# GpSimd normalises the fourth and fifth block's x and makes four low parts of the first two blocks; the engines' programs in a new order

## What is computed

```
x = x + layernorm(attention(layernorm(x)))       # one head: q, k, v from W_qkv, softmax(q k' / sqrt(128)) v
x = x + layernorm(ffn(layernorm(x)))
ffn(h): h = silu(h w1' * s1) * (h w2' * s2)      # 128 -> 512, weights -1, 0 or 1, a scale for each output
        h = gelu(h h1' * s3)                     # 512 -> 512
        h = gelu(h h2' * s4)                     # 512 -> 512
        return h w3' * s5                        # 512 -> 128
```

## Time and profile before

| | |
|---|---|
| median of 3 timed runs | 129.98 us (129.56 to 130.08) |
| profiled execution | 130.0 us |
| its span, first to last instruction | 127.8 us |
| TensorE matmuls busy | 122.6 us, 96% |
| VectorE busy | 103.3 us, 81% |
| ScalarE busy | 97.4 us, 76% |
| GpSimd busy | 27.9 us, 22% |
| granted TensorE clock, mean | 1.0 of full speed |

### The profile page before, as it was taken

The page is one execution under the profiler, slowest core; times in us unless marked ns, Lnnn a source line. Parts: engine busy times, 40 slices in busy tenths (PEclk is TensorE's granted clock), DMA queues, the critical chain, the costliest instruction groups (busy, mean ns, idle before and its releaser), DMA issues.

```text
span 127.8 us, 2356 instructions
## 1 busy us (share of the span) xinstructions
PE 122.6 (96%) x698; PEld 102.5 (80%) x698; DVE 103.3 (81%) x337; ACT 97.4 (76%) x182; POOL 27.9 (22%) x40
## 2 busy tenths in 40 slices
PE   7999999999999999999999999999999999999980
PEld 5585979989778988887889888888888788899970
DVE  0697789998898997888798998458999895695853
ACT  4248887987999739599899189799992996997520
POOL 3294220033300015230000054400001550000351
PEclk9999999999999999999999999999999999999999
DMA  4899999100000000010000000010000002000003
GB/s 106 250 308 379 381 375 373 33 5 3 0 0 5 0 5 0 3 41 0 0 5 0 0 5 0 16 68 0 8 0 0 0 5 82 0 5 0 0 29 100
DMA packets 5344, 8.28 MB, mean 65 GB/s; under 512 B 465, under 2 KB 2769, under 8 KB 5329
## 3 DMA queue, kind: packets, MB, share of 16 engines
q1 hardware_dynamic: 3840, 5.12, 12.6%
q0 software_dynamic: 1344, 2.88, 6.7%
q10 hardware_dynamic: 144, 0.07, 0.2%
HBM read 7.02 MB, written 1.05 MB: 63 GB/s over the span
## 4 chain that ended last, share of the span: by engine, by line
PE 84%; DVE 6%; DMA 3%; ACT 1%; SPq 1%; issue 1%; DVEq 0%; ACTq 0%
PE F L1181 22%; PE F L1187 22%; PE A L1090 5%; PE A L1058 5%; PE F L1130 5%; PE F L1137 5%; PE A L1187 3%; PE A L1181 3%; DMA xs<-x 3%; PE A L1041 3%; PE A L1074 2%; PE A L1029 2%; DVE xn_odd L653 2%; PE F L1210 1%; PE A L1222 1%
## 5 line engine op out<-in xcount | busy, mean ns | idle before, releaser
L319 POOL TENSOR_TENSOR rstd<-mv,minus_half 128x4 f32<-128x4 f32 (+1 forms) x19 | 17.7, 935 | 87.1 <-DVE mv L637 87.0
L1181 PE MATMUL F<-a_hi,h_hi 128*128 128x512 f32 (+1 forms) x152 | 35.5, 355 | 0.0
L630 DVE TENSOR_TENSOR a_lo<-act_full,a_hi 128x512 fp32r<-128x512 f32 (+1 forms) x52 | 30.6, 602 | 5.9 <-ACT act_full L432 5.2
L1187 PE MATMUL F<-a_lo,h_hi 128*128 128x512 f32 (+1 forms) x152 | 34.9, 352 | 0.0
L440 ACT ACTIVATE a_hi<-F,sc 128x512 fp32r<-128x512 f32 (+1 forms) x33 | 20.5, 632 | 12.2 <-PE F L1187 12.2
L1187 PEld LDWEIGHTS F<-a_lo,h_hi 128*128 128x128 f32 x152 | 25.7, 189 | 4.0
L1181 PEld LDWEIGHTS F<-a_hi,h_hi 128*128 128x128 f32 x152 | 25.2, 189 | 3.6 <-issue 0.2
L432 ACT ACTIVATE act_full<-F,sc 128x512 f32<-128x512 f32 (+1 forms) x38 | 23.1, 621 | 1.7 <-PE F L1187 1.7
L733 DVE SCALAR_TENSOR_TENSOR act_full<-F,sc,silu 128x512 f32<-128x512 f32 (+1 forms) x16 | 10.7, 676 | 1.0 <-ACT silu L421 0.8
L421 ACT ACTIVATE silu<-F,sc 128x512 f32<-128x512 f32 (+1 forms) x16 | 9.8, 633 | 1.1 <-PE F L1137 0.9
L1130 PE MATMUL F<-x2T_hi,w_hi 128*128 128x512 f32 (+1 forms) x32 | 10.3, 405 | 0.1
(11 more groups left out here) (158 smaller groups left out, 198.5 us busy)
## 6 DMA issues: line engine op xcount, KB each, us to landing
h_raw<-h SPq DMA_DIRECT2D x2, 1024.0 KB, 11.2
h_hi<-h POOLq DMA_DIRECT2D x2, 1024.0 KB, 12.1
xs<-x SPq DMA_DIRECT2D x3, 256.0 KB, 3.9
out<-outs SPq DMA_DIRECT2D x3, 256.0 KB, 2.1
w_raw<-w SPq DMA_DIRECT2D x1, 512.0 KB, 6.4
w_hi<-w POOLq DMA_DIRECT2D x1, 512.0 KB, 7.3
xs<-x SPq DMA_DIRECT2D x2, 128.0 KB, 8.9
w_raw<-w SPq DMA_DIRECT2D x1, 256.0 KB, 16.1
```

The costliest lines, as they stand in the source:

```text
L319: nc.gpsimd.tensor_tensor(rstd[:, ln, tiles(b)], mv[:, ln, tiles(b), 1], minus_half[:, 0:SIZES[b]], ALU.pow).then_inc(rstd_ready[ln], 1)
L630: nc.vector.tensor_tensor(dst, full, hi.bitcast(f32), ALU.subtract).then_inc(done, 1)
L1181: nc.tensor.matmul(out, terms[k][0], terms[k][2], start=(k == 0), stop=False)
L1187: last = [nc.tensor.matmul(out, terms[k][0], terms[k][3], start=False, stop=(k == KT - 1)) for out, terms in groups]
```

## The change

GpSimd gets ten instructions that were DVE's. `POOL_LO` gives it the first group's low part of A2 and of A3 in blocks 0 and 1. A new function x_normalised on GpSimd makes the normalised x of blocks 3 and 4, four tiles and two tiles, with a semaphore of its own (xn_by_pool); DVE's x_normalised(3) and (4) go. The lists of all four computing engines are changed in many places, mostly by exchanging neighbours. The core of the diff:

```
+        xn_by_pool = sem("xn_by_pool")
...
-        POOL_LO = ((0, 0, 0, 0, 0), (0, 0, 0, 0, 0), (0, 0, 0, 0, 0))
+        POOL_LO = ((0, 0, 0, 0, 0), (1, 1, 0, 0, 0), (1, 1, 0, 0, 0))
...
+            def x_normalised(b):
+                if b > 2:
+                    pool.wait_ge(xT_in_psum, b - 1)
+                pool.wait_ge(rstd_ready[LN_X], b + 1)
+                for t in range(SIZES[b]):
+                    n = T0[b] + t
+                    nc.gpsimd.tensor_scalar(lane(b).xn[:, t, :], xs[:, n, :], mv[:, LN_X, n, 0:1], rstd[:, LN_X, n:n + 1],
+                                            ALU.subtract, ALU.mult).then_inc(xn_by_pool, 1)
...
                 for t in range(SIZES[b]):
-                    pe.wait_ge(xn_ready, T0[b] + t + 1)
+                    if b < 3:
+                        pe.wait_ge(xn_ready, T0[b] + t + 1)
+                    else:
+                        pe.wait_ge(xn_by_pool, T0[b] - T0[3] + t + 1)
...
             silu(0, 1)
             v_copy(2)
+            pT_copy(1, 1)
             silu(0, 2)
-            pT_copy(1, 1)
             silu(0, 3)
```

More of the change, by code:

```diff
@@ L352, in _ @@
             rsqrt(LN_O, 1)
+            lo_part(A2, 0, 0)
             rsqrt(LN_X1, 1)
+            lo_part(A3, 0, 0)
             rsqrt(LN_X, 3)
+            x_normalised(3)
             rsqrt(LN_X, 4)
+            x_normalised(4)
+            lo_part(A2, 1, 0)
+            rsqrt(LN_Y, 0)
             rsqrt(LN_O, 2)
-            rsqrt(LN_Y, 0)
+            rsqrt(LN_X1, 2)
             last_add(0)
-            rsqrt(LN_X1, 2)
+            lo_part(A3, 1, 0)
             rsqrt(LN_O, 3)
@@ L853, in _ @@
             x_statistics(3)
-            low(A3, 0, 0)
             x2T_low(1)
-            x_normalised(3)
             maxima(2, 1)
+            low(A3, 0, 1)
+            low(A3, 0, 2)
             pT_copy(2, 0)
-            low(A3, 0, 1)
             gate(1, 0)
             gate(1, 1)
-            low(A3, 0, 2)
+            high(A1, 1, 0)
+            low(A1, 1, 0)
+            high(A1, 1, 1)
+            x_statistics(4)
             low(A3, 0, 3)
-            high(A1, 1, 0)
-            high(A1, 1, 1)
-            low(A1, 1, 0)
             pT_copy(2, 1)
             squared_sums(2)
+            gate(1, 2)
             low(A1, 1, 1)
-            gate(1, 2)
             high(A1, 1, 2)
@@ L875, in _ @@
             low(A1, 1, 3)
+            xT_copy(3)
             attention_out(2)
-            x_statistics(4)
-            xT_copy(3)
-            low(A2, 1, 0)
             low(A2, 1, 1)
@@ L919, in _ @@
             low(A3, 2, 0)
-            x_normalised(4)
+            low(A3, 2, 1)
             x2T_low(3)
             xT_copy(4)
-            low(A3, 2, 1)
+            low(A3, 2, 2)
             gT_copy(4)
             v_copy(4)
-            low(A3, 2, 2)
+            low(A3, 2, 3)
             gate(3, 0)
             maxima(4, 0)
-            gate(3, 1)
-            low(A3, 2, 3)
             high(A1, 3, 0)
             low(A1, 3, 0)
+            gate(3, 1)
+            high(A1, 3, 1)
             pT_copy(4, 0)
-            high(A1, 3, 1)
+            squared_sums(4)
+            low(A1, 3, 1)
             gate(3, 2)
-            low(A1, 3, 1)
             high(A1, 3, 2)
@@ L946, in _ @@
             y_shifts(2)
+            low(A2, 3, 0)
             x1_normalised(4)
-            low(A2, 3, 0)
             low(A2, 3, 1)
+            x2T_low(4)
             low(A2, 3, 2)
-            x2T_low(4)
-            shift_x1(4)
             low(A2, 3, 3)
@@ L955, in _ @@
             gate(4, 1)
+            w3_scale()
             high(A1, 4, 0)
+            high(A1, 4, 1)
             gate(4, 2)
@@ L1288, in _ @@
             up_high(1, 2)
+            up_low(1, 2)
             up_high(1, 3)
-            up_low(1, 2)
             up_low(1, 3)
@@ L1317, in _ @@
             probs_transposes(3, 0)
+            up_high(2, 3)
             up_low(2, 2)
-            up_high(2, 3)
+            up_low(2, 3)
             probs_transposes(3, 1)
-            up_low(2, 3)
             end(A3, 1, (0,), 3)
```

94 lines of the change are left out of this document (45 added, 49 removed).

## The result

The changed kernel takes 131.84 us (median of 4 runs, 131.61 to 132.25), the kernel before, timed beside it, 129.77 (129.36 to 130.08). The ratio is 1.0159, with a 95% interval of 1.0135 to 1.0183: the change makes the kernel 2.1 us slower. The profiled run took 131.95 us, of which 130.1 is span and 1.85 lies around it; before it was 130.0, 127.8 and 2.2.

What follows compares the result with a forecast made beforehand. TensorE, busy 122.6 of 127.8 us, was taken to bound the kernel, so only its waits count. Gains of 0.20 and 0.20 from 130.0 gave 129.6, range 128.7 to 130.8.

Steps and rivals of the forecast that it cites:

- the lock: Large GpSimd SBUF operations hold two-input DVE operations, possibly reaching TensorE at 57 to 60.4 us: 0, ends 0 and 1.1.
- The lock bites: Rival: at 57 to 61 us GpSimd gets in first twice, TensorE waits 1.1 us for x2T_low(2); 130.8, chance 0.18.
- the o_shift row: At 53.81 DVE's o_shift took 0.73 instead of 0.15, ending with GpSimd's last_add(0); evidence for the lock.
- the two even: low(A2,1,0) on GpSimd can hold x1_block(2)'s chain by 0.7 or so; o_shift's 0.58 loss goes: about even.
- signs of being wrong: Late x2T_low(2), DVE low parts of 1 us or more beside GpSimd's, GpSimd normalisations over 0.74, other waits in first 11 us.
- the first term: Third block's scores around 25.6 us: ACT copies pT(1,1) before silu(0,2); gain 0.20, ends 0.40 and 0.
- second term: x_normalised(3) to GpSimd, 36 to 40 us: attend(2,0) and the next transposes earlier; gain 0.20, ends 0.40 and -0.10.
- the 0.05 taken off: Part of the 0.25 gain at the transposes given back, through x_statistics(4) before pT_copy(2,1) and high(A1,1,2); leaves 0.20.
- More comes back: Rival: all waits between 25 and 40 us go, 1.3 us; 128.7, chance 0.20.
- my upper end of 0.74: Price of one GpSimd normalisation: bounded by 0.26 below and 0.74 above, taken as 0.5.
- The cover: GpSimd's four normalisations end by 37.2 or 38.2, before transposes need them: no cost, 2 us of cover at the dear end.
- the rest of the order: keep_warm, v and g projections and later lists move work where TensorE does not wait: zero, within 0.1 either way.

Runs made afterwards that it cites:

- Low part back on VectorE: Changed kernel with only low(A3,1,0) back on VectorE, between x1_block(2) and x1_normalised(2): 130.66 us, ratio to the kernel before 1.0075.
- both at once: Changed kernel with low(A3,1,0) back on VectorE, and y_normalised(0) and last_add(0) at their places before: 130.56 us, ratio to the kernel before 1.0065.
- The two fastest versions: Changed kernel, last_add(0) at its place before, block 1's low parts back on VectorE: 129.65 us; block 0's back too: 129.58 us.
- x_normalised(3) alone: Kernel before with one edit, x_normalised(3) on GpSimd behind rsqrt(LN_X,3) instead of on VectorE: 130.17 us beside 129.79, ratio 1.0031.
- one collision in the kernel before: Kernel before with one edit, low(A3,1,0) moved from VectorE to GpSimd behind rsqrt(LN_X1,2): 130.46 us beside 129.90, ratio 1.0048.

## Why the prediction was wrong

The forecast was 129.6, the range 128.7 to 130.8; the kernel takes 131.84. The chance for slower was 0.16.

**The step that failed is the lock, taken as 0.** GpSimd held x1_normalised(2) for 1.48 us (2.60 instead of 1.12), and TensorE ended 1.44 later for it. The place and both GpSimd instructions were the ones named in the rival "The lock bites"; x2T_low(2), at which the rival had TensorE wait, ended at 61.23, and its matmuls followed at 61.86 without a wait. Three things in the working of the lock were wrong.

First, which instructions can be held. I read the o_shift row as one about two-input operations and priced only low parts. What was held were x1_normalised(2)'s instructions, with one tile as input. The Trainium skill, SBUF — State Buffer, "Who interferes with whom", has this: besides operations with two SBUF inputs it says that `tensor_scalar` can run in a two-port mode that shares the pair with GpSimd, and that whoever issues first holds it for the whole instruction. The prediction quoted the first half of it. The trace agrees with the second in that the instruction is held to the other's end: 0.85 and 1.30 against 0.34, each ending 0.08 after GpSimd's. It does not show who issued first: the first of the two has its recorded start 0.03 before last_add(0) (57.09 and 57.12). That `tensor_scalar` ran in the two-port mode no run shows. The roles exchanged, a two-input low part holding GpSimd's rsqrt, gave 1.36 against 1.01. Where the opening says of the engines that they meet only through semaphores, that is too strong. The trace of before had the hold of a normalisation too, on VectorE and GpSimd at 10 us, where a normalisation took 0.68 beside GpSimd's issue of a transfer:

```profile
9.97 0.68 DVE L653 TENSOR_SCALAR xn_even<-xs,mv,rstd 128x128 f32<-128x128 f32 x1
...
9.84 0.75 POOL L312 DMA_DIRECT2D h_hi<-h  x1
```

Second, where VectorE would be. I put x1_normalised(2) through at 57.4, since o_shift would lose 0.58 less. Two paragraphs earlier I had said that lo_part(A2,1,0) would cost the same chain about as much. I called the two even and then used only the gain. The normalisation began at 56.83 as before, and met both GpSimd instructions. With that low part taken back, and last_add(0) at its place before, it began at 56.02. This term, held to be even, is what was left of the loss in "both at once".

Third, the argument against the rival: "DVE's own instructions overlap, so there is hardly a moment in which GpSimd can get in". GpSimd got in twice, between instructions that follow each other without a gap. And where there was a gap, in front of the first, it got in as well ("Low part back on VectorE").

The size then follows. The held normalisations stand directly in front of TensorE, not two low parts away from it, so 1.5 us of hold cost 1.44 at TensorE's end and not the 1.1 of the rival. Without the two GpSimd instructions about 1 us of the loss goes; the rest stays until the chain is on time again. Of the signs of being wrong, two came: low(A2,1,1) took 1.38 beside lo_part(A2,1,0), and GpSimd's normalisations took 0.80.

**The gains.** The low terms of A1's last part start at 26.93 instead of 27.07, 0.14 of the 0.20 that the first term had. Of the second term, attend(2,0) at 36.48 and the transposes at 39.81 (forecast 39.83) came as worked out:

```profile
26.93 0.50 PE L1200 MATMUL F<-a_lo,h_hi 128*128 128x256 f32 x2
...
36.48 1.16 PE L1103 MATMUL A<-v_even,pT_even 128*128 128x128 f32 x8
37.77 0.69 PE L1143 MATMUL F<-x2T_hi,w_hi 128*128 128x512 f32 x2
...
39.81 0.66 PE L1087 MATMUL A<-ident,probs_even 128*128 128x128 f32 x4
```

But x2_transposes(2) starts at 57.58 instead of 57.66: of 0.40 forecast, 0.08 was left. One part of this is the sum itself. The second term was worked out in times of the trace of before, and the exponentials that it ends on do not move with the first term; so 39.83 instead of 40.08 is the whole lead at that point, with the 0.20 of the first term in it, and the two should not have been added. By its own working the forecast was 129.8. The other part is given back, and the 0.05 taken off for it was too little: attend(2,1), behind the copy to pT_even that now stands behind x_statistics(4) and low(A3,0,3) and ends at 41.29, starts at 41.34 instead of 41.46, so 0.12 is left there of the 0.27 at 39.81. The two fastest versions agree: their median spans, 127.6 and 127.75, are that of the kernel before, 127.7. This speaks against "More comes back" too.

**Prices.** GpSimd's normalisations take 0.80 each, above my upper end of 0.74; this group's mean holds one of 1.03:

```profile
L342 POOL TENSOR_SCALAR xn_odd<-xs,mv,rstd 128x128 f32<-128x128 f32 x4 | 3.4, 853 | 0.2 <-POOL rstd L320 0.2
```

The cover held: the last ends at 37.96, and its transposes come at 42.34. The low parts cost 0.74 and 1.27 to 1.29, close to what was put. All orders together, without the new GpSimd work, gave a ratio of 1.0014; the rest of the order, put at zero, was not tested apart from the order of the first term.

**The tail** was in no term of the prediction. One small item more: last_add(2) beside low(A2,3,2), which takes 1.03 at 105.22, makes TensorE wait 0.3 there.

## What to carry to other kernels

Before you move work to GpSimd, list the VectorE instructions that will run beside it with SBUF alone as operands, one-input `tensor_scalar` among them, and ask which of them TensorE waits for next. Then price the hold from the moment at which the VectorE instruction wants to start to the end of the GpSimd instruction, and the whole length of the latter as the upper end: 0.41 was lost of one of 0.74, 0.89 of one of 1.29, 1.48 of both in a row. An idle slot of VectorE beside a small GpSimd instruction can be the better place: low(A3,1,0) had been free in it, starting just behind the rsqrt. Where it started 0.16 ahead of it, the rsqrt took 0.35 longer. When two terms of one chain are called even, carry both to the next step.

## What the hardware showed that was not expected

GpSimd's one-input normalisation did not hold VectorE's two-input low part: at 34.98 one took 0.41 beside it, as it does alone. The reverse was seen: the GpSimd instruction that started 0.06 us after a low part's start took 1.03 instead of 0.79.

The time outside the span differs between kernels and mostly little between runs of one: 2.11 to 2.28 in the kernel before, 1.75 to 1.85 in the changed one, 2.34 to 2.43 with x_normalised(3) alone; but 1.76 to 2.15 with one collision in the kernel before. A comparison of kernels to within 0.3 us has to look at both parts. What sets it was not tested.
